# One half-chunk in fourteen groups of gathered rows, fetched row by row from two other queues

## The reference

```python
agg = segment_sum(h[src], dst)                       # layer 0 (GIN): then two matmuls with batch norms
a_in  = segment_sum(feat_in[src] * iw, dst)          # layer 1: two weighted sums, then gates
a_out = segment_sum(feat_out[dst] * ow, src)
agg = segment_sum(x[edge_col], edge_row)             # layer 2 (GIN)
h = relu(concat(x_i, x_j - x_i) @ W1 + b1)           # layer 3: a product per edge,
msg = h @ W2 + b2; out = segment_sum(msg, tgt) / deg # then the mean over the edges of a target
```

## Time and profile before

| what | us |
|---|---|
| median of 3 runs | 3427.59 |
| the profiled execution, span from first to last instruction (the profile has no other time of it) | 4205.1 |
| GpSimd busy | 2373.5 (56%) |
| TensorE busy | 2930.9 (70%) |
| VectorE busy | 2117.9 (50%) |
| ScalarE busy | 1141.1 (27%) |

### The profile page before, as it was taken

The page is one execution under the profiler, slowest core; times in us unless marked ns, Lnnn a source line. Parts: engine busy times, 40 slices in busy tenths (PEclk is TensorE's granted clock), DMA queues, the critical chain, the costliest instruction groups (busy, mean ns, idle before and its releaser), DMA issues. The chain is left out here.

```text
span 4205.1 us, 55362 instructions
## 1 busy us (share of the span) xinstructions
PE 2930.9 (70%) x11580; PEld 1849.8 (44%) x11581; DVE 2117.9 (50%) x6459; ACT 1141.1 (27%) x3023; POOL 2373.5 (56%) x2458
## 2 busy tenths in 40 slices
PE   3677776555542846677588887755554899988989
PEld 1233333333321434444333332433333548888878
DVE  6566664333320455444456655533333576667664
ACT  1466661000000330000000000300000356666662
POOL 3544445666667046666666666666666226666662
PEclk6788887667665867888799999976676999999999
DMA  3000002333320043333366666433333136666664
GB/s 123 2 1 1 1 1 74 90 89 90 90 56 2 20 139 88 101 106 105 109 176 180 177 176 178 138 89 89 87 91 86 34 124 186 187 188 185 189 187 143
DMA packets 184321, 438.94 MB, mean 104 GB/s; under 512 B 53924, under 2 KB 78623, under 8 KB 184233
## 3 DMA queue, kind: packets, MB, share of 16 engines
q0 software_dynamic: 135568, 372.32, 31.3%
q1 hardware_dynamic: 48665, 65.55, 4.7%
HBM read 403.39 MB, written 34.24 MB: 104 GB/s over the span
## 5 line engine op out<-in xcount | busy, mean ns | idle before, releaser
L834 POOL DMA_INDIRECT acc<-table,stg_idx x1170 | 1128.5, 965 | 767.8 <-issue 349.1
L2116 PE MATMUL psum<-acc,oh 128*128 x2600 | 871.4, 489 | 637.7 <-issue 456.5
L2116 PEld LDWEIGHTS psum<-acc,oh 128*128 128x128 f32 x2600 | 598.2, 244 | 912.3 <-issue 821.2
L1497 DVE TENSOR_TENSOR acc<-acc,psum 128x257 f32 (+1 forms) x660 | 276.0, 418 | 962.7 <-remote 565.4
L1032 ACT CAST stg_idx<-rec 128x2 int32 (+1 forms) x784 | 148.4, 193 | 2113.0 <-remote 841.2
L945 POOL DMA_INDIRECT TT<-qtable,stg_row x440 | 424.1, 964 | 282.4 <-PE psum L2428 150.9
L860 POOL DMA_INDIRECT H<-gtable,stg_idx x391 | 379.1, 970 | 199.5 <-issue 116.5
L2205 PE MATMUL psum<-H 125*128 125x440 bf16 x1600 | 375.5, 399 | 154.2 <-issue 48.2
L2137 PE MATMUL psum<-H,oh 128*128 x880 | 426.2, 630 | 79.8 <-issue 31.1
L810 POOL DMA_INDIRECT recs<-acc,sst_idx x290 | 284.6, 981 | 338.1 <-ACT acc L977 255.6
L2428 PE MATMUL psum<-oh,TT 128*128 128x128 f32 x3520 | 444.3, 277 | 34.7 <-issue 26.0
(11 more groups left out here) (277 smaller groups left out, 3210.7 us busy)
## 6 DMA issues: line engine op xcount, KB each, us to landing
acc<-table,stg_idx POOLq DMA_INDIRECT x1173
TT<-loc_dram SPq DMA_DIRECT2D x22, 320.0 KB
TT<-qtable,stg_row POOLq DMA_INDIRECT x440
Wm<-loc_dram SPq DMA_DIRECT2D x22, 320.0 KB
H<-gtable,stg_idx POOLq DMA_INDIRECT x391
gtable<-H SPq DMA_DIRECT2D x24, 256.0 KB
qtable<-H SPq DMA_DIRECT2D x24, 256.0 KB, 2.2
table<-H SPq DMA_DIRECT2D x8, 640.0 KB
```

Source lines behind the costliest of these rows:

```text
L834: pool.indirect_dma_start(out=dst[:, c, 0:D], out_offset=None, in_=src, in_offset=bass.IndirectOffsetOnAxis(ap=stg_idx[:, c:c + 1], axis=0 ...
L1497: V.tensor_tensor(at, at, sum_bank(j)[:, 0:w], ALU.add).then_inc(added, 1)
L2116: last = mm(sum_bank(j)[:, 0:w], oh[:, 2 * j + k, :], rows_flat[:, ds(start[j] + k * S, w)], start=(k == 0), stop=(k == 1))
```

## The change

In each narrow pass the groups are taken by `DUO` = 14 (two rounds of the ring), 14 such duos in a pass. In each duo but the first, the second half-chunk of the seventh group (`ROWED` = 6) is no longer gathered by GpSimd. Its 128 rows are fetched one DMA per row into one of two new places beside the ring: rows 0 to 63 by SyncE, rows 64 to 127 by ScalarE. They are fetched one duo ahead, 4 or 5 rows after each of the duo's 14 groups, on both queues. The node numbers come from a table `seat_rows`, made once for each edge order by a transpose on TensorE and two DMAs, and are loaded into registers 16 at a time. TensorE's second address now comes from a third table, `second_tab`, which VectorE makes ahead of pass 0 (`second_halves`, nine operations on 1 x 220 values for each of the two orders). `relay` counts `arrived` for the seventh group only when the fetched rows have landed too. GpSimd's DMA scratch is set to 8192 bytes of a partition (its default is 16384), which makes room.

```diff
+            def row_fetcher(eng, engine, turn, o, duo, q):
+                on_act = engine == mybir.EngineType.Activation
+                held = [None]
+                def fetch(step, steps=DUO):
+                    for k in range(LANES * step // steps, LANES * (step + 1) // steps):
+                        if k % SEATS == 0:
+                            held[0] = loads(engine, seats_of(o, on_act), duo * LANES + k, SEATS, N - 1)
+                        lane = k + (LANES if on_act else 0)
+                        eng.dma_start(rows_flat[lane:lane + 1, (2 * RING_G + q) * S:(2 * RING_G + q) * S + D],
+                                      table[ds(held[0][k % SEATS], 1), :]).then_inc(rows_landed[turn][q], 16)
...
+            def relay_duo(turn, o, duo, q, uses, fetch):
+                for step in range(DUO):
+                    r, j = step // RING_G, step % RING_G
...
+                    sp.wait_ge(landed[j], landed_count(turn, duo, r, j) - (16 if ends else 0))
+                    if step == ROWED and uses is not None:
+                        sp.wait_ge(rows_landed[turn][q], uses * (P * 16))
                     sp.sem_inc(arrived, 1)
+                    if fetch is not None:
+                        fetch(step)
...
-                with pool.Fori(n * GITS, (n + 1) * GITS - 1) as i:
-                    for j in range(RING_G):
-                        gather_pair(i, j, src, dst)
+            def gather_duo(n, duo, rowed, src, dst):
+                for step in range(DUO - 1 if isinstance(duo, int) and duo == DUOS - 1 else DUO):
+                    j = step % RING_G
+                    chunks = (2 * j,) if rowed and step == ROWED else (2 * j, 2 * j + 1)
+                    gather_group(duo * DUO + (n * GROUPS + step), j, src, dst, chunks)
...
+                def stage_duo(duo, q):
+                    fetch = fetcher(duo, q)
+                    for r in range(2):
+                        freed = loads(mybir.EngineType.Activation, free_tab[PASSES[n][0]],
+                                      duo * DUO + (r - 1) * RING_G, RING_G, PAIRS)
+                        for j in range(RING_G):
+                            act.wait_ge(summed, freed[j] + (n * PAIRS + SP_IT))
+                            stage_group(n, duo * DUO + (r * RING_G + j), j)
+                            fetch(r * RING_G + j)
...
+            src = wait_filled(act, "rows0", 0)
+            nc.scalar.copy(turned_rows[:, :], src[0:DUOS - 1, 0:P]).then_inc(emptied[bank("rows0", 0)], 1)
+            wait_emptied(act, "rows0", 0)
+            move_seats(act, 0)
+            act.wait_ge(seats_loaded, 32)
...
+            def second_halves(o, scratch):
+                at = acc[32 * o:32 * o + 1, scratch:scratch + 2 * PAIRS].bitcast(i32).rearrange("p (t u) -> p t u", t=2)
...
+                second = loads(mybir.EngineType.PE, second_tab[o], at, SP_IT, (2 * RING_G + 1) * S)
...
-                        last = mm(sum_bank(j)[:, 0:w], oh[:, 2 * j + k, :], rows_flat[:, ds(start[j] + k * S, w)],
+                        last = mm(sum_bank(j)[:, 0:w], oh[:, 2 * j + k, :], rows_flat[:, ds((start, second)[k][j], w)],
...
-    nc = bacc.Bacc("TRN2", target_bir_lowering=False, num_devices=1)
+    nc = bacc.Bacc("TRN2", target_bir_lowering=False, num_devices=1, dynamic_dma_scratch_size=8192)
```

More of the change, by code:

```diff
@@ L27 @@
 GITS = GROUPS // RING_G
+DUO = 2 * RING_G
+DUOS = GITS // 2
+ROWED = RING_G - 1
+LANES = P // 2
+SEATS = 16
 ITERS = (GROUPS + NB - 1) // SP_IT
@@ L86 @@
 assert FOLD_AT + 6 < ITERS
+assert DUOS * DUO == GROUPS and DUOS % 2 == 0 and LANES % SEATS == 0
 def rows(t):
@@ L410, in gnn_kernel @@
         consts = sem("consts")
+        second_ready = sem("second_ready")
+        rows_turned = sem("rows_turned")
+        seats_loaded = sem("seats_loaded")
+        rows_landed = [sems(f"rows_landed{t}_", 2) for t in range(3)]
         stages_begun = sem("stages_begun")
@@ L716, in _ @@
             weight(W1e, "L3_gnn_W1", w_loaded[3])
-            relay(3, 2)
+            sp.wait_ge(seats_loaded, 64)
+            relay(1, 2)
             b, c = jobs["down2"][-1]
@@ L1039, in stage_first, with stage_round, stage_rest, fetcher @@
                     stage_group(n, j, j)
[L1041 to L1047, removed]
+            def stage_round(n, i, fetch):
+                freed = loads(mybir.EngineType.Activation, free_tab[PASSES[n][0]], (i - 1) * RING_G, RING_G, PAIRS)
+                for j in range(RING_G):
+                    act.wait_ge(summed, freed[j] + (n * PAIRS + SP_IT))
+                    stage_group(n, i * RING_G + j, j)
+                    if fetch is not None:
+                        fetch(j, RING_G)
+            def stage_rest(n, turn):
+                def fetcher(duo, q):
+                    return row_fetcher(act, mybir.EngineType.Activation, turn, PASSES[n][0], duo, q)
+                def stage_duo(duo, q):
[3 more added lines that the diff above has]
+                                      duo * DUO + (r - 1) * RING_G, RING_G, PAIRS)
+                        for j in range(RING_G):
+                            act.wait_ge(summed, freed[j] + (n * PAIRS + SP_IT))
+                            stage_group(n, duo * DUO + (r * RING_G + j), j)
+                            fetch(r * RING_G + j)
+                stage_round(n, 1, fetcher(0, 1))
+                with act.Fori(0, DUOS // 2 - 1) as b:
+                    stage_duo(b * 2 + 1, 0)
+                    stage_duo(b * 2 + 2, 1)
+                for i in (GITS - 2, GITS - 1):
+                    stage_round(n, i, None)
             def stage_wide():
@@ L2056, in pick_index, with turn_rows @@
                 done(last, f"pick_i{o}", 0)
+            def turn_rows(o, field):
+                wait_emptied(pe, f"pick_i{o}", 0)
+                dst = take_bank(f"rows{o}", 0)
+                first = 2 * (DUO + ROWED) + 1
+                done(nc.tensor.transpose(dst[0:DUOS - 1, 0:P], recs[o][:, first:first + 2 * DUO * (DUOS - 2) + 1:2 * DUO, field],
+                                         ident[:, :]), f"rows{o}", 0)
             def transpose_group(layer, g):
@@ L2213, in _ @@
             transposes(0)
+            turn_rows(0, 3)
+            pe.wait_ge(second_ready, 1)
             drained("z0")
```

120 lines of the change are left out of this document (86 added, 34 removed).

## The result

The changed kernel takes **3547.78 us** (median of 4 runs, 3546.4 to 3548.43) against 3427.51 before (4 runs, 3425.26 to 3429.46) on the same chip: ratio 1.035, 95% interval 1.0337 to 1.0362, that is 120.3 us slower. The forecast was slower, at 3650, with a range of 3395 to 3860.

The account below looks back on a forecast made before the run. GpSimd's gathers and the gaps where staging waits bound the narrow passes; with the change ScalarE's row issues would set the pace: 3427.6 + 219 + 5 = 3652, rounded to 3650 us, range 3395 to 3860.

Parts of the forecast that it names:

- The step that sized a row: On ScalarE's queue: one row costs 0.45 us with its register operation, so 64 rows take 28.8 us a duo.
- I take these stalls for the price of recording: Long register operations in the profile of before: put down to recording, explaining gaps of some 340 us in all.
- 410 us, 1.05 us a gather: GpSimd's narrow pass in a timed run of before: the middle taken between 385 and 425 us a pass.
- at 1.26 a gather, 340 of the 777.5 us would have no place: Argument against GpSimd staying the bound: the profiled gather pace could not explain the shorter timed median.
- 35 us: ScalarE's duo in a timed run: middle of 29 and 40.7 us, giving +73 us a pass, +219 in three.
- In the profiled execution 40.7 against 39.5, nearly no change: Narrow passes as profiled: ScalarE's duo against 27 gathers, in us, giving 569 us a pass against 572.6.
- Small terms: VectorE's 18 operations and the transpose, copy and DMAs ahead of ScalarE's loop: together +5 us.
- TensorE's third load at zero: In narrow passes: 57 us a pass of queue time, covered while TensorE waits for rows, so counted as zero.
- Scratch at zero: GpSimd's halved DMA scratch: never more than 14 half-chunks outstanding and an even pace, so counted as zero.
- Rival 1: GpSimd stays the bound and the change pays, with ScalarE's duo below 28.4 us: 3392 us, chance 0.17.
- Rival 3: SyncE's and ScalarE's row issues cannot overlap, 37 to 42 us a duo: 3920 us, chance 0.07.
- Rival 2: TensorE's third register load becomes the wait, 57 us more a narrow pass: 3557 us, chance 0.13.

Follow-up runs that it names:

- before_again: The kernel before, unchanged, profiled a second time: 4210.98 us, span 4209.3; its timed runs on that chip took 4205 to 4233 us.
- rows_none: The changed kernel without any row fetch or wait for one; third load, tables and scratch kept: 4167.27 us, ratio 0.9896 to before; made again, 4226.08 us, 0.9904.
- rows_const: The changed kernel with rows read from fixed table addresses, without their register loads and register operations; all issues and waits kept: 3392.39 us, ratio 0.9894 to before.
- third_load: The kernel before with one more register load on TensorE in each iteration of its narrow passes, 132 in all: 4277.64 us, ratio 1.0022 to before.
- rows_28_2: The changed kernel with rows fetched only for every second duo, 128 spread over 28 groups, in the quick condition: 3440.61 us, ratio 1.0034 to before.

## Why the prediction was right and where it was wrong

**Right: the mechanism, and the sign.** ScalarE's row issues stand ahead of the staging copies, and its sum per duo exceeds 27 gathers. The terms of that sum, forecast and measured in the change's pass 0:

| per duo, on ScalarE | forecast, us | measured, us |
|---|---|---|
| 64 rows | 64 x 0.45 = 28.8 | 64 x 0.37 = 23.7, and 4 x 0.27 for the first row after a load = 1.1 |
| register loads | 6 x 1.54 = 9.2 | 4 x 1.21 + 2 x 1.74 = 8.3 |
| 14 staging copies | 2.7 | 2.8 |
| the loop's way back | none | 2.6 every second duo = 1.3 |
| sum | 40.7 | 37.2 |

The duo itself takes 38.2. The step that sized a row leaned on an issue of 0.29 to 0.333 us; a one-row issue is 0.213, shorter than any row of before.

The size is another matter: +222 us were forecast and +120 measured, and two wrong inputs went into it.

**Wrong: "I take these stalls for the price of recording", and with it "410 us, 1.05 us a gather".** No price of recording shows (`before_again`), and a gather is 1.26 us in both conditions. The 777.5 us between the profile of before and its timed median were another condition of the chip. Laid side by side, the profiles of before and of the change have them in the staging of records ahead of pass 0 (592 us there, 391 in the profile after), in the stretch ahead of pass 1 (137 and 3), in the fifth stretch (696 and 610) and, some 80 us each, in the four passes (the wide one 578.7 and 494.9), where I had sought the most of them. I had written that "at 1.26 a gather, 340 of the 777.5 us would have no place". That was a slip: 340 is what the gaps explain, and 437 were left. They had a place too, 201, 134 and 86 us of them in the three stretches without a gather from `table` named here, which I never laid out.

**"35 us" for ScalarE's duo** was a middle between a value that shrinks with the passes and 40.7. Nothing shrank. It lies near 38.2 by luck, and the excess came from the other side: I set it against 28.4 us for 27 gathers and found 6.6 a duo; measured it is 38.2 against 34.0, so 4.2. That difference of 2.4 us over 39 duos is most of the 100 us by which the forecast was too high. The sign held because both inputs were wrong the same way: with a gather at 1.26 and ScalarE still at 35, the method gives 13 x 35 + 34 = 489 us a pass against 493, and no slowdown. With the sum 40.7, not shrunk, it gives 13 x 40.7 + 34 = 563, +210 in three. With the measured 38.2 it gives 531, and with 17 us at the start, less some 4 of it that the 531 hold already, about 543 against the measured 540. The sum of one queue per duo is the right model for the steady part; its errors were in the inputs.

**The forecast for the same condition was wrong too, and by more.** "In the profiled execution 40.7 against 39.5, nearly no change", span 4180 to 4350, passes of 560 to 610. Measured 4747 us, passes of 744, 740 and 743: 54.6 us a duo. (The profile after, in the quick condition, has 540, 534 and 527.) I had read that 46-ns register operations stall for up to 1207 ns on TensorE and priced 128 new ones a duo on ScalarE and as many on SyncE at their medians. The stalls moved to the queues that issue the rows. That is also why SyncE, whose rows add nothing to ScalarE's in the quick condition, is full in this one.

**Small terms.** +5 forecast; 120 less the 116 in the passes leaves 4. TensorE's third load at zero: 9 us (3 to 15) in the stalling condition. Scratch at zero: nothing shows, in `rows_none` and in `rows_const`. "The wide pass is unchanged": 494.9 us, where `rows_const` has 494.1.

**The rivals.** Rival 1 (3392 us, "a row at 0.25 to 0.34") did not happen for the change, but for `rows_const`, where a row costs ScalarE's queue 0.295 from one to the next and the loads are gone: 3392.39. That the two times agree so closely is luck, since the rival's 41 us saved go by 1.05 us a gather; at 1.26 it is 49, of which 37 were seen. Rival 3 is out: an issue lasts 213 ns beside SyncE's issues and without them. The Trainium skill's page Perfetto Trace Analysis, section DMA Instruction — HWDGE (DVE, Sync), has one generator shared by the DVE and Sync sequencers and locked for one at a time; it doesn't name ScalarE. If that held for ScalarE and SyncE, an issue would have taken up to 0.213 + 0.225 = 0.44 us as an estimate, and no such wait shows in these rows. Rival 2 is out by `third_load` and `rows_const`. The Trainium skill's page DMA: Bandwidth & Descriptors, section Latency and other measured facts, has about 600 ns as the floor of a register load. The least in the profile after is 552 ns, the median of sixteen registers 1.21 us on ScalarE, so the trace's value was the one to take.

## What to carry to other kernels

Before a profile is used to price a change, lay its span beside the timed median, and where they differ compare all stretches, those without the operation in question too; don't put the difference down to recording without a second profile. Work moved off a bound engine onto a queue is to be summed per turn of the ring, with its register loads, its address operations and its loop branch, and compared with what the bound engine takes for one turn: here 0.37 us of address work and issue for a 1-KB row, 64 times on each of two queues, replaced one 1.26-us gather. If an idle queue is to carry such work, take care with the one whose next instruction frees the bound engine: what it needs for a turn has to stay below what the bound engine needs, as in `rows_28_2` behind the start of each pass.

## What the runs showed of the hardware that I had not expected

- **Two conditions of a chip.** One chip had the kernel before at 4210.07 us (7 runs) and, four minutes later, at 3429.71 (7 runs). In the stalling one, register, move, branch and semaphore instructions of TensorE, SyncE or ScalarE stall for about 0.7 us, and GpSimd's gathers keep their 1.26 us. The change is +3.5% in one and +11.3% in the other. What sets the condition stays open, and so does what picks the queue: TensorE has 433 such stalls before and 39 in the change.
- **The way back of a long loop.** ScalarE's loop over two duos has some 500 instructions, and each way back costs it 2.4 to 3.0 us; without the rows' register instructions it has some 220, and a way back takes 0.17 to 0.23. Fifteen of them are about 39 of the quick condition's 120 us lost, if all lie on the path. The page counts what the instruction queue fetched, first in the change, then in `rows_const`:

```profile
q14 instruction: 235, 1.93, 0.2%
```
```profile
q14 instruction: 65, 0.53, 0.0%
```

  The Trainium skill's page Runtime: NRT & Kernel Launch, section Instruction fetch mechanics, says that a taken branch whose target isn't in the two pages at hand must fetch it first; more packets where the way back is long agree with that. No run here took the way back alone away.
- **A one-row issue is cheap, its address isn't.** 213 ns on ScalarE and 225 on SyncE for the DMA instruction, 0.37 to 0.41 with the address. At a fixed address the DMA instruction takes 265 and 248 ns and 0.295 from one to the next, with nothing else:

```profile
L600 SPq DMA_DIRECT2D acc<-table x2496: 211/248/369, 442.4 to 2529.3; - x192
L600 ACTq DMA_DIRECT2D acc<-table x2496: 200/265/517, 449.2 to 2517.9; - x192
```
